# Three node updates of a graph network: norm steps, squares, one product's wait and two late operations moved

## The reference

```python
# layer 0: update of a node from itself and the mean of its messages
updated = relu(concat([h, agg_sum / clip(counts, 1)]) @ W_upd + b_upd);  x = x + updated
# layer 1: sum of neighbours (scaled by degrees) and the node itself
x = x + ((aggregated + h) @ W.T + b)
# layer 2: after attention over edges
agg = agg @ Wo + bo                      # then gamma, beta from the task embedding
t = layer_norm(h + agg, ln1_g, ln1_b)
y = layer_norm(t + gelu(t @ W1 + b1) @ W2 + b2, ln2_g, ln2_b);  x = x + y
# after each of them, for the next layer
h = relu(layernorm(x))                   # mean, centred, variance, 1/sqrt, scale
```

## Time and profile before

| | us |
|---|---|
| three runs, median (lowest to highest) | 4822.12 (4820.42 to 4827.02) |
| profiled execution, its own time | 4793.24 |
| its span, first to last instruction | 4791.4 |
| mean granted TensorE clock | 0.649 |
| PE, DVE, ACT, POOL busy | 3037.5, 2708.5, 916.2, 2762.8 |

### The profile page before, as it was taken

One profiled execution on the slowest core, in us unless ns is written; L12 is line 12 of the kernel. 1 busy time (PEld: TensorE's weight loads), 2 busy tenths in 40 slices (PEclk: granted clock), 3 DMA queues, 4 the chain that ended last, 5 costly groups with the idle time before them and its releaser, 6 DMA issues. The chain is left out here.

```text
span 4791.4 us, 53751 instructions
## 1 busy us (share of the span) xinstructions
PE 3037.5 (63%) x12326; PEld 1838.8 (38%) x12326; DVE 2708.5 (57%) x6253; ACT 916.2 (19%) x1645; POOL 2762.8 (58%) x2438
## 2 busy tenths in 40 slices
PE   3564745655797899664777657777646665555424
PEld 1222534544665687441222224545312222222113
DVE  7997742222457444675777727777745554444323
ACT  0332410000122000221222214334212221111100
POOL 0673057777111673446777678888157776877631
PEclk8876655555767555555555568787578887677655
DMA  6333621111455111542222244444111121333215
GB/s 255 79 71 121 268 82 24 24 24 23 114 158 152 34 26 25 177 177 87 41 41 43 35 72 91 107 87 105 65 45 36 37 38 30 32 28 30 24 14 109
DMA packets 337039, 363.11 MB, mean 76 GB/s; under 512 B 236961, under 2 KB 268843, under 8 KB 336864
## 3 DMA queue, kind: packets, MB, share of 16 engines
q1 hardware_dynamic: 219890, 261.52, 16.7%
q0 software_dynamic: 94096, 80.65, 13.9%
q10 hardware_dynamic: 22878, 18.95, 1.2%
HBM read 174.93 MB, written 201.00 MB: 78 GB/s over the span
## 5 line engine op out<-in xcount | busy, mean ns | idle before, releaser
L801 PE MATMUL e_ps<-e_msg,e_hot 128*128 x2408 | 571.4, 424 | 222.9 <-issue 213.0
L801 PEld LDWEIGHTS e_ps<-e_msg,e_hot 128*128 128x128 f32 x2408 | 530.1, 329 | 301.8 <-issue 301.8
L1767 POOL DMA_INDIRECT u_a<-attended,dst_end x392 | 489.3, 1248 | 149.9 <-issue 119.1
L2401 PE MATMUL d_pl<-d_hot,d_fields 128*65 128x512 f32 x712 | 479.8, 836 | 0.0
L774 DVE TENSOR_TENSOR sums<-e_ps,sums 128x455 f32 (+1 forms) x172 | 108.1, 628 | 557.2 <-PE e_ps L801 557.2
L719 POOL DMA_INDIRECT e_msg<-from_src,e_src x200 | 192.5, 962 | 286.2 <-DMA e_first<-lot_first 227.2
L2345 POOL DMA_INDIRECT flows<-d_out,d_end x160 | 263.6, 1648 | 107.1 <-issue 104.7
L1424 ACT ACTIVATE u_zt<-u_pt 128x256 f32<-128x256 f32 (+1 forms) x392 | 164.2, 433 | 840.4 <-PE u_pt L1319 838.8
L2056 POOL DMA_INDIRECT list<-s_rec,s_place x200 | 200.6, 1003 | 212.5 <-DVE s_place L1972 156.5
L2332 POOL DMA_INDIRECT d_near<-term,d_rec x196 | 191.0, 975 | 194.3 <-DMA d_rec<-list 135.1
L724 POOL DMA_INDIRECT e_msg<-h1d,e_src x200 | 204.9, 1025 | 120.3 <-issue 60.6
(11 more groups left out here) (383 smaller groups left out, 7249.3 us busy)
## 6 DMA issues: line engine op xcount, KB each, us to landing
x<-sums SPq DMA_DIRECT2D x28, 896.0 KB, 7.8
u_x<-x SPq DMA_DIRECT2D x28, 896.0 KB, 5.7
terms<-s_zeros SPq DMA_DIRECT2D x16, 812.5 KB
s_key_row<-src_key SPq DMA_DIRECT2D x50, 256.0 KB
term<-u_h SPq DMA_DIRECT2D x14, 910.0 KB, 3.7
flows<-s_zeros SPq DMA_DIRECT2D x14, 896.0 KB
n_x<-in_x SPq DMA_DIRECT2D x14, 896.0 KB
h<-n_h SPq DMA_DIRECT2D x14, 896.0 KB
```

What stands on the lines that cost most here:

```text
L801: last = nc.tensor.matmul(to, hot[s][:, q, :], rows, start=False, stop=q == LOT - 1)
L1767: pool.indirect_dma_start(A[s][:, j, :], None, net.attended[:, :], bass.IndirectOffsetOnAxis(ap=net.dst_end[:, tile:tile + 1], axis=0)).th ...
L2401: last = nc.tensor.matmul(pl[0:WEIGHT + 1, :], fields[:, j, :], hot[:, j, :], start=j == 0, stop=j == J - 1)
```

## The change

Four edits, all inside `node_update`.

1. Norm steps of updates 0 and 1: total behind evacuation 0 instead of 4, variance behind 2 instead of 0, scaling behind 4 instead of 2, sums or row means behind 5 instead of 3, centring behind 6 instead of 5.
2. ScalarE in updates 0 and 1: the square of a group stands behind the first copy of the group after next in the norm's order, instead of at the end of the group before; the root behind copy 3 instead of copy 1.
3. Update 0: GpSimd's product waits for `inputs_used` of the group two back, which frees its half of `Z`, and no longer for the load; TensorE waits for the load itself.
4. Update 2: gain product and tail add go behind the last evacuation of `attend` and behind its signal; the variance of the second norm in `mlp` goes from behind evacuation 5 to behind 6.

```diff
@@ TensorE
                         if layer == 0:
+                            pe.wait_ge(loaded[c[1]], 16 * in_loads * (c[2] + 1))
                             fill(nc, net, unread, 5)
@@ ScalarE
                             copy((c[0], c[1]), i, new is None)
-                            if i == 1 and old is not None:
+                            if i == 0 and old is not None:
+                                square(old[0])
+                            elif i == 3 and old is not None:
                                 root(old[0])
-                        if new is not None:
-                            square(new[0])
...
-                    root(LAST - 1)
-                    square(LAST)
-                    root(LAST)
+                    for r in (LAST - 1, LAST):
+                        square(r)
+                        root(r)
@@ VectorE, norm_step
-                        if i == 0 and old is not None:
+                        if i == 0 and new is not None:
+                            total(summed(new[0]))
+                        elif i == 2 and old is not None:
                             variance(old[0])
-                        elif i == 2 and old is not None:
+                        elif i == 4 and old is not None:
                             if layer == 0:
                                 scale_twice(old)
...
-                        elif i == 3 and old is not None:
+                        elif i == 5 and old is not None:
                             if layer == 0:
                                 begin_sums(old)
                             else:
                                 row_means(old)
-                        elif i == 4 and new is not None:
-                            total(summed(new[0]))
-                        elif i == 5 and new is not None:
+                        elif i == 6 and new is not None:
                             centre(summed(new[0]))
@@ VectorE, attend of update 2
-                            if t is not None and i == 3:
-                                v.drain()
-                                nc.vector.tensor_tensor(TG[t[1]][:, :, :], T[t[1]][:, :, :], channels(net.norms[:, 0, :]), ALU.mult)
-                            if x is not None and i == 4:
-                                v.drain()
-                                nc.vector.tensor_tensor(X[x[1]][:, :, :], X[x[1]][:, :, :], H[x[1]][:, :, 0:C], ALU.add).then_inc(tail_ready, 1)
                         v.drain()
                         if c is not None:
                             v.sem_inc(inputs_used, 1)
+                        if t is not None:
+                            nc.vector.tensor_tensor(TG[t[1]][:, :, :], T[t[1]][:, :, :], channels(net.norms[:, 0, :]), ALU.mult)
+                        if x is not None:
+                            nc.vector.tensor_tensor(X[x[1]][:, :, :], X[x[1]][:, :, :], H[x[1]][:, :, 0:C], ALU.add).then_inc(tail_ready, 1)
+                        v.drain()
@@ VectorE, mlp of update 2
-                                elif i == 5:
+                                elif i == 6:
                                     variance(2 * y[0] + 1, 1)
@@ GpSimd, update 0
-                    with pool.Fori(0, SUPER // 2) as t:
-                        for s in range(2):
-                            pool.wait_ge(loaded[s], 16 * in_loads * (t + 1))
-                            pool.wait_ge(deg_ready, 2)
-                            nc.gpsimd.tensor_tensor(Z[s][:, :, C:P], summed(2 * t + s), ...
+                    pool.wait_ge(deg_ready, 2)
+                    for number in range(SUPER):
+                        if number > 1:
+                            pool.wait_ge(inputs_used, number - 1)
+                        nc.gpsimd.tensor_tensor(Z[number % 2][:, :, C:P], summed(number), ...
```

More of the change, by code:

```diff
@@ L1724, in _ @@
                 if layer == 0:
-                    with pool.Fori(0, SUPER // 2) as t:
-                        for s in range(2):
-                            pool.wait_ge(loaded[s], 16 * in_loads * (t + 1))
-                            pool.wait_ge(deg_ready, 2)
-                            nc.gpsimd.tensor_tensor(Z[s][:, :, C:P], summed(2 * t + s),
-                                                    inv_count[:, bass.ds(G * (2 * t + s), G)].unsqueeze(2).to_broadcast([P, G, C]), ALU.mult).then_inc(z_ready, 1)
+                    pool.wait_ge(deg_ready, 2)
+                    for number in range(SUPER):
+                        if number > 1:
+                            pool.wait_ge(inputs_used, number - 1)
+                        nc.gpsimd.tensor_tensor(Z[number % 2][:, :, C:P], summed(number),
+                                                inv_count[:, G * number:G * (number + 1)].unsqueeze(2).to_broadcast([P, G, C]), ALU.mult).then_inc(z_ready, 1)
                 elif layer == 1:
```

## The result

| | before | after |
|---|---|---|
| timed runs, median (lowest to highest), 4 each | 4823.32 (4820.42 to 4827.02) | 4795.79 (4789.64 to 4798.62) |
| ratio | | 0.9941 [0.9924, 0.9958] |
| profiled execution, its own time | 4793.24 | 4789.64 |
| span, granted clock | 4791.4, 0.649 | 4787.9, 0.648 |

The two rows of time disagree: timed, the change saves 28 us of 4823, and in the two profiled executions it saves 3.6. Before is a program with two kinds of execution, and its trace came from the rarer one. Of five profiles with the code of before in update 2, that trace alone has the stage in 719 us; the other four have 744 to 752. The timed runs fit this, but part less sharply: 12 of 78 in the experiments took 4796 to 4815 us, the others 4818 to 4841, and none was as short as the profiled 4793.24.

The account below looks back on a forecast made before the run. Bounds: VectorE and TensorE by turns in update 0, mostly low clock and a boundary wait in update 1, GpSimd's gather issues in update 2. Terms -22 + 22 - 3 = -3 us, carried to the median: 4819 us, range 4790 to 4842.

Parts of the forecast that it names:

- rival B: Update 0: the clock holds and four more slow groups turn fast; -20 in all, 4802 us; chance 0.20.
- Update 0, fast group and boundary: New norm order: fast group 14.4 us instead of 16.3, boundary -1.05; six pairs -17.7, stage end +0.6.
- Update 0, the clock (-5): Smaller gaps let the clock survive a boundary, one slow group turning fast; -5 us, bounds 0 to -33.
- Rival A: Update 0 gives nothing, as the clock falls inside fast groups at ScalarE's stops; +19 in all, 4841 us; chance 0.22.
- TensorE's wait for the load (0): Update 0: the load is issued about 2 us later but read a whole group later; cost 0.
- Update 1: Centring held up by GpSimd's less_mean product; a group 21.15 us against 19.24; +22 us, bounds -12 to +26.
- rival C: Update 1: GpSimd doesn't get in first, every group takes 18.55 us; -37 in all, 4785 us; chance 0.12.
- Update 2 (b), the variance: Second norm's variance behind evacuation 6 lengthens VectorE's chain in the tail; +3 us.
- Update 2 (a), the move (-6): Gain product and tail add side by side stretch gather issues 1.85 us a group against 2.40; -6, bounds -10 to +8.
- The carry to the median: The shown runs' median, 4822.12, lies 28.9 us above the profiled execution; that difference was carried over to the forecast.

Follow-up runs that it names:

- second pair: Profiles of the kernel before and of the changed kernel, both run again without any edit; ratios to the kernel before 1.0006 and 0.9955.
- e12: The kernel before with only update 0's new order of norm steps, square and root; GpSimd's product still waits for the load: 4816.95 us, 0.9987.
- e7: The kernel before with only update 0's waits changed (GpSimd's product for the buffer, TensorE for the load): 4825.11 us, 0.9997.
- e4: The kernel before with all edits of update 0 and none of the others: 4811.79 us, 0.9962.
- e3: The changed kernel with update 1's centring behind evacuation 5 and row means behind 6: 4753.81 us, 0.9855.
- e6: The kernel before with only the variance of update 2's second norm moved behind evacuation 6: 4837.30 us, 1.0017.
- e8: e3 with the variance of update 2's second norm back behind evacuation 5: 4740.24 us, 0.9821 of the kernel before.
- e5: The kernel before with only update 2's gain product and tail add moved behind the last evacuation of attend: 4787.00 us, 0.9915.
- e1: The kernel before, unchanged, timed against itself and profiled again: 4827.86 us, 1.0006.

## Why the prediction was right, and where it wasn't

The number (4819) has the result in its range, 4790 to 4842, but not in its own narrower one (4809 to 4829), and the timed difference, -24 and -28 us, was called "faster" with a chance of 0.38 only. That the wide range holds it is luck in part: its lower end made room for rival B, a clock that holds in update 0, and what made the kernel faster was a clock that holds in update 2, which no term had. The sum of -3 meets the profiled -3.6 by chance, as said above; the three stages gave +3.9 there and -28.7 in the second pair. Step by step:

- **Update 0, fast group and boundary: right in size, one cause wrong.** Forecast -17.7 + 0.6 without the clock's part; -16.3 in the first pair, -16.0 in the second. Groups of 14.25 us (14.4), the second evacuation 4.40 us behind the first (4.8), no block of the small product. But the 1.43 us of that block were put down to GpSimd's earlier start, and e12 reaches fast groups of 14.1 to 14.3 us without it: it is the scaling's later slot that leaves the block behind. e7, with the earlier start alone, gains nothing.
- **Update 0, the clock (-5): didn't come.** The gap shrank from 3.17 to 2.64 us, not to 1.8, and in the profile of after each of the five groups from the third on that ran wholly at the high clock, up to the twelfth, is followed by one at 0.50 to 0.58; the mean over the stage went from 0.729 to 0.740. Rival A, too, is out: it needed a mean near 0.68, and e4 is faster.
- **TensorE's wait for the load (0): nothing was seen of it.** e7 has both waits in and is not slower.
- **Update 1: right in mechanism, a little high.** +18.7 in the first pair and +17.2 in the second for +22; a period of 20.99 for 21.15, a centring of 4.59 for 4.6, started 0.47 us behind GpSimd for 0.4. What was off is the start: the first two groups took 18.8 us for 25.7, 6.9 saved instead of 3.4; the end cost 6.2 us for 4. What rival C would have won is there to be had, and more: e3 has 17.3 a group where C had 18.55.
- **Update 2 (b), the variance: right where it was looked for, too small as a whole.** The tail grew by 3.2 us for 3. But e6 and e8 put the variance's new place at 11 to 13 us of update 2. That it "sat in a slot that VectorE idled in anyway" was read from the old place. Where the passes are at the high clock most of the cost lies in the gathers, and not in a wait: no issue of after waits for anything, but its 392 issues are busy 487.48 us, for 478.61 in e5, which differs from it in update 2 by the variance alone. Which VectorE operation meets an issue at another point there, and stretches it more, is not known.
- **Update 2 (a), the move (-6): the term that failed.** Its stretch of the gathers was near in the group shown (2.06 us for 1.85), and too cautious as a whole: the move by itself takes 10.7 us off the gathers of the quick profile and 12.1 off those of e1. What failed is that the stage was taken as bound by GpSimd in every execution. That holds in the profiled one only. In most executions of before TensorE runs ten of the fourteen MLP passes at 1.2 GHz, the groups take up to 49.8 us for gathers of 44 to 47, and the VectorE/TensorE chain is the bound, on which the moved operations stood. There the whole of update 2 is worth -30 instead of -3 (750.7 to 720.8), -43 from the move and +13 from the variance.
- **The carry to the median: the same fault.** The profiled execution was 29 us faster than the median, and this was added as a constant. It was no constant: 31.5 us of such a difference stand in the very stage that the change touches, and the change removes them (-29.9 there in the second pair). Only after's profile, which is typical for it (4789.64; median 4795.79), could be carried over so.

The timed parts add up to that account: update 0 -18 (e4), the move -39, the variance +11 (e6), and update 1's +17 from the traces make -29; after as a whole was timed at -24 and -28. Each timed part is known to about 10 us either way, so the agreement shows that no large part is missing, and no more.

What stays open: what decides which kind an execution of before becomes. Both kinds run the same instructions, and what first lets the clock fall, in the third pass in e1 (in e4, e7 and e12 too), is not known. How the move keeps the clock up isn't either. A denser run of TensorE's work in the attention pass is an obvious guess, but the traces don't bear it out: TensorE was busy 10.3 to 13.6 us of an attention pass in the first profile of before, with the high level in the passes behind, and 10.6 to 13.6 us in e1, mostly with the low one. The runs show that the move does it, and that more multiplications at the start of a pass do it as well.

## What to carry to other kernels

Before pricing a change, hold the profiled execution against the median of the timed runs: where they differ by more than the effect sought, the profile may be of a rarer kind, and each term should be worked out for the other kind too, with TensorE at its low clock and whatever then becomes the bound. A moved VectorE operation with two SBUF inputs should be laid against GpSimd's product to the tenth of a microsecond: a start 0.47 us too late cost 2.57 us in the operation itself and, with the square left uncovered, 3.7 us a group. Two steps side by side are worth trying in either order. And where a stage has a tail behind the engine that seems to bound it, look at the tail's length too: a chain that falls behind shows there first, while the bounding engine still never waits.

## What the runs showed of the hardware that was not expected

- The same program has two kinds of execution on one core, parted by TensorE's granted clock in one stage: MLP passes in 19.9 us at 0.85, or 25.4 at 0.50; update 2 in 719 or 751 us. By the Trainium skill ("TensorE: Matmul & The Clock Gate", section "What's actually happening") the number of multiplications at the low clock at a kernel's start varies from run to run of the same kernel, and this costs under 1% of a typical kernel span. Here the variation stands far behind the start, in update 2, and is of that size (31.5 us of 4791 are 0.7%), which is still more than this change is worth.
- Four multiplications whose result is not read, at the start of each pass, are worth 32 us against the slow kind (783.1 to 750.7), and eight bring 12 of 14 passes to the high level (719.9, in one profile each), though they add work to TensorE.
- Moving two VectorE operations, with no change to TensorE's instructions, took TensorE's busy time in update 2 from 581.9 us (e1) to 521.1 (e5).
- A VectorE operation that asks during GpSimd's 3.19 us product ended 1.87 us after it in after (1.88 in the earlier trace rows). Gather issues took 2.33 and 1.63 us beside VectorE operations with two SBUF inputs, 0.95 without, as in the earlier trace rows. That such operations leave the issue of DMAs alone, as the Trainium skill infers ("SBUF — State Buffer", section "Who interferes with whom"), is contradicted again: moving two of them took 12 us off the busy time of the same 392 issues, from 490.65 to 478.61.
